# Gather stage of a graph layer on one Trainium2 core: VectorE makes a pick between two adds, the valid mask is folded into the scaling of keys and values, and ScalarE normalises the pairs' rows

## The reference

```python
xn = layernorm(x)
x = x + gcn(xn, edge_index, edge_weight) + mix(xn)     # both read xn
x = x + ffn(layernorm(x))                              # 8 experts, top 2
# gcn: per node the sum over its edges of weight * xw[source], then a two-layer head
# mix: q, k, v = split(xn @ w_qkv); k, v = ln(k), ln(v) by head
#      kv = k^T v / N by head (a 32x32 matrix); out = q @ kv; then a two-layer head
```

## Time and profile before

| | us |
|---|---|
| median of three runs | 4517.35 |
| profiled execution | 4502.67 |
| its span | 4500.9 |
| TensorE busy | 3399.5 (76%) |
| VectorE busy | 2931.0 (65%) |
| GpSimd busy | 2770.0 (62%) |
| ScalarE busy | 1429.0 (32%) |

### The profile page before, as it was taken

The page is one execution under the profiler, slowest core; times in us unless marked ns, Lnnn a source line. Parts: engine busy times, 40 slices in busy tenths (PEclk is TensorE's granted clock), DMA queues, the critical chain, the costliest instruction groups (busy, mean ns, idle before and its releaser), DMA issues. The chain is left out here.

```text
span 4500.9 us, 75623 instructions
## 1 busy us (share of the span) xinstructions
PE 3399.5 (76%) x20283; PEld 2597.3 (58%) x20283; DVE 2931.0 (65%) x7496; ACT 1429.0 (32%) x4439; POOL 2770.0 (62%) x2543
## 2 busy tenths in 40 slices
PE   7677777246777777777756777777777589999995
PEld 6455554243444444444435666566665479999885
DVE  8899998674565565655655555555555665555676
ACT  2455554440111111111002222222322255555442
POOL 0488888436666666666666666666666245555553
PEclk9678787557888888888868888888888799999998
DMA  2111111763333333333334444444446612222466
GB/s 76 17 3 3 3 3 3 239 228 116 110 108 111 110 112 108 111 110 111 109 89 119 128 131 131 130 130 132 128 130 121 139 46 70 68 70 68 148 217 215
DMA packets 285822, 472.50 MB, mean 105 GB/s; under 512 B 95011, under 2 KB 180778, under 8 KB 285743
## 3 DMA queue, kind: packets, MB, share of 16 engines
q0 software_dynamic: 140544, 273.69, 24.5%
q1 hardware_dynamic: 138047, 193.90, 12.7%
q10 hardware_dynamic: 7154, 3.99, 0.3%
HBM read 350.11 MB, written 123.70 MB: 105 GB/s over the span
## 5 line engine op out<-in xcount | busy, mean ns | idle before, releaser
L1621 POOL DMA_INDIRECT rows<-table,idx x1664 | 1675.1, 1007 | 815.5 <-issue 497.3
L1904 DVE TENSOR_TENSOR acc<-acc,ps_seg 128x256 f32 x1664 | 695.5, 418 | 955.5 <-remote 761.6
L2069 PE MATMUL ps_seg<-rows,pick 128*128 128x256 f32 x3328 | 997.3, 429 | 272.0 <-DVE acc L1904 182.0
L2069 PEld LDWEIGHTS ps_seg<-rows,pick 128*128 128x128 f32 x3328 | 660.4, 213 | 514.0 <-issue 404.6
L771 POOL DMA_INDIRECT records<-sort_rec,sort_addr x280 | 528.8, 1889 | 260.7 <-DVE sort_rec L874 158.7
L1746 DVE TENSOR_SCALAR pick<-iota_row,loc,ewt 128x128 f32<-128x128 f32 x1680 | 529.2, 363 | 5.6 <-remote 1.8
L2509 POOL DMA_INDIRECT y_rows<-arena,idx x212 | 249.8, 1178 | 290.0 <-DVE arena L2556 185.2
L2641 PE MATMUL ps_h<-arena,up_now 128*128 128x128 f32 x3392 | 417.8, 277 | 0.0
L2625 PE MATMUL ps_y<-down_now,arena 128*128 128x256 f32 x1696 | 401.4, 380 | 0.0
L2641 PEld LDWEIGHTS ps_h<-arena,up_now 128*128 128x128 f32 x3392 | 398.3, 193 | 1.9
L926 PE MATMUL ps_out<-acc 128*128 128x240 bf16 x1568 | 281.5, 364 | 142.0 <-DVE acc L860 141.9
(11 more groups left out here) (385 smaller groups left out, 5122.7 us busy)
## 6 DMA issues: line engine op xcount, KB each, us to landing
rows<-table,idx POOLq DMA_INDIRECT x1664
acc<-y_rows SPq DMA_DIRECT2D x28, 640.0 KB
xn<-xn_dram SPq DMA_DIRECT2D x100, 128.0 KB
table<-acc SPq DMA_DIRECT2D x98, 128.0 KB
xT_dram<-xT SPq DMA_DIRECT2D x98, 128.0 KB
xn<-xT_dram SPq DMA_DIRECT2D x49, 256.0 KB
skip<-skip_dram SPq DMA_DIRECT2D x49, 256.0 KB
x_rows<-acc SPq DMA_DIRECT2D x49, 256.0 KB
```

What stands on the lines that cost most here:

```text
L1621: pool.indirect_dma_start(out=rows[:, t, :], out_offset=None, in_=k.table, in_offset=bass.IndirectOffsetOnAxis(idx[:, h, t:t + 1], 0), bou ...
L1904: dve.tensor_tensor(here, here, sums(u), ALU.add).then_inc(added[u], 1)
L2069: last = pe.matmul(sums(t), pick[:, h, t, :], rows[:, t, :], start=True, stop=True)
```

## The change

On VectorE the order of picks and adds becomes pick, add, pick, add; the wait for the pair's sums stands ahead of its first add, behind the first pick. The multiplication by `valid` goes; the scaling takes it as a second factor, in one instruction with three operands. Normalising the pairs' rows goes from VectorE, at the end of a step, to ScalarE, in the next step between `aggregated` and `features`, as rows * rstd + shift, for which VectorE makes shift = -mean * rstd.

```diff
 def normalised(i):                                   # now ScalarE's
+    start_after(act, rows_out, 16 * i)
+    start_after(act, f_done, i)
+    act.wait_ge(shift_done, i + 1)
+    act.sem_inc(head_held, 1)
+    for h in both:
+        act.activation(xl[:, h:h + 1, :], k.acc[:, bass.ds(2 * i + h, 1), :], ACT.Identity,
+                       scale=rstd[:, h:h + 1], bias=shift[:, h:h + 1]).then_inc(xl_done, 1)
...
                         if due(i - 2):
+                            normalised(i - 2)
                             features(i - 2)
...
                 def inverses(m):
                     dve.wait_ge(k_sd, m + 1)
+                    start_after(dve, k_scaled, m)
                     dve.reciprocal(rs[:, :], sd[:, :]).then_inc(k_rs, 1)
-                def masked(m):
-                    dve.wait_ge(k_rs, m + 1)
-                    dve.tensor_scalar(rsv[:, :], rs[:, :], k.valid[:, bass.ds(m, 1)], None, ALU.mult).then_inc(k_rsv, 1)
-                def scaled(m, u):
-                    dve.wait_ge(k_rsv, m + 1)
                     dve.wait_ge(k_raw, m + 1)
                     start_after(dve, k_summed, m - 1)
-                    dve.tensor_tensor(kv_heads(u), by_head4(raw[:, u, :]),
-                                      rsv[:, :]..., ALU.mult).then_inc(k_scaled, 1)
+                    dve.scalar_tensor_tensor(
+                        out=kv_heads(u), in0=by_head4(raw[:, u, :]), scalar=k.valid[:, bass.ds(m, 1)],
+                        in1=rs[:, :]..., op0=ALU.mult, op1=ALU.mult).then_inc(k_scaled, 1)
...
                 def inverse(i):
                     dve.wait_ge(std_done, i + 1)
+                    start_after(dve, xl_done, 2 * i)
                     dve.reciprocal(rstd[:, :], std[:, :]).then_inc(rstd_done, 1)
-                def normalised(i):
-                    start_after(dve, rows_out, 16 * i)
-                    start_after(dve, f_done, i)
                     dve.wait_ge(rstd_done, i + 1)
                     dve.sem_inc(head_held, 1)
-                    for h in both:
-                        dve.tensor_scalar(xl[:, h:h + 1, :], k.acc[:, bass.ds(2 * i + h, 1), :], mv[:, h, 0:1],
-                                          rstd[:, h:h + 1], ALU.subtract, ALU.mult).then_inc(xl_done, 1)
+                    dve.scalar_tensor_tensor(out=shift[:, :], in0=mv[:, :, 0], scalar=-1.0, in1=rstd[:, :],
+                                             op0=ALU.mult, op1=ALU.mult).then_inc(shift_done, 1)
...
                     for t in range(STEP_TILES):
                         make_pick(1 - h, t)
+                        if t % 2 == 0:
+                            dve.wait_ge(summed_up[t // 2], n + 1)
+                        if t > 0:
+                            dve.wait_ge(added[t - 1], n + 1)
+                        else:
+                            start_after(dve, added[ALL_TILES], n)
+                        here = acc_row[:, bass.ds(places[t], D)]
+                        dve.tensor_tensor(here, here, sums(t), ALU.add).then_inc(added[t], 1)
                         if t % 2 == 0:
                             continue
-                        dve.wait_ge(summed_up[t // 2], n + 1)
-                        for u in (t - 1, t):
-                            if u > 0:
-                                dve.wait_ge(added[u - 1], n + 1)
-                            else:
-                                start_after(dve, added[ALL_TILES], n)
-                            here = acc_row[:, bass.ds(places[u], D)]
-                            dve.tensor_tensor(here, here, sums(u), ALU.add).then_inc(added[u], 1)
```

More of the change, by code:

```diff
@@ L1449, in gather_and_mix @@
         rstd = sb("rstd3", [P, 2])
+        shift = sb("shift3", [P, 2])
         wr = sb("wr", [P, DC, N_EXPERTS])
@@ L1455, in gather_and_mix @@
         rs = sb("rs", [P, 2 * HEADS])
-        rsv = sb("rsv", [P, 2 * HEADS])
         kv = sb("kv", [P, 2, 2 * DC, WIDE])
@@ L1497, in gather_and_mix @@
             k.sem(name) for name in "idx_done loci_done loc_done ewt_done gather_held".split())
-        (kv_consts, k_turned, k_xT, k_kv, k_raw, k_sq, k_ss, k_sd, k_rs, k_rsv, k_scaled, k_summed, k_all_summed) = (
-            k.sem(name) for name in ("kv_consts k_turned k_xT k_kv k_raw k_sq k_ss k_sd k_rs k_rsv k_scaled k_summed "
+        (kv_consts, k_turned, k_xT, k_kv, k_raw, k_sq, k_ss, k_sd, k_rs, k_scaled, k_summed, k_all_summed) = (
+            k.sem(name) for name in ("kv_consts k_turned k_xT k_kv k_raw k_sq k_ss k_sd k_rs k_scaled k_summed "
                                      "k_all_summed").split())
@@ L1503, in gather_and_mix @@
         (mix_hid, gelu_done, mix_out, h7_done, h7T_done, h7T_copied, gcn_hid, relu_done, all_out, x1_done, stats_done, mv_done,
-         std_done, rstd_done, xl_done, f_done, fT_copied, lg_done, lgb_done, eps2_made, head_held) = (
+         std_done, rstd_done, shift_done, xl_done, f_done, fT_copied, lg_done, lgb_done, eps2_made, head_held) = (
             k.sem("pair_" + name) for name in (
                 "mix_hid gelu_done mix_out h7_done h7T_done h7T_copied gcn_hid relu_done all_out x1_done stats_done mv_done "
-                "std_done rstd_done xl_done f_done fT_copied lg_done lgb_done eps2_made held").split())
+                "std_done rstd_done shift_done xl_done f_done fT_copied lg_done lgb_done eps2_made held").split())
         by_block = lambda a: a.rearrange("(t p) d -> p t d", p=P)
@@ L1683, in deviation, with normalised @@
                     act.activation(std[:, :], mv[:, :, 1], ACT.Sqrt, bias=eps2[:, :], scale=1.0 + EPS).then_inc(std_done, 1)
+                def normalised(i):
+                    start_after(act, rows_out, 16 * i)
[5 more added lines that the diff above has]
+                                       scale=rstd[:, h:h + 1], bias=shift[:, h:h + 1]).then_inc(xl_done, 1)
                 def features(i):
@@ L1765, in inverses, with scaled @@
                     dve.wait_ge(k_sd, m + 1)
+                    start_after(dve, k_scaled, m)
                     dve.reciprocal(rs[:, :], sd[:, :]).then_inc(k_rs, 1)
[L1768 removed]
+                def scaled(m, u):
                     dve.wait_ge(k_rs, m + 1)
[L1770 to L1773 removed]
                     dve.wait_ge(k_raw, m + 1)
                     start_after(dve, k_summed, m - 1)
[L1776 to L1778 removed]
+                    dve.scalar_tensor_tensor(
+                        out=kv_heads(u), in0=by_head4(raw[:, u, :]), scalar=k.valid[:, bass.ds(m, 1)],
+                        in1=rs[:, :].rearrange("p (c h) -> p c h", c=2 * DC).unsqueeze(3).to_broadcast(
+                            [P, 2 * DC, HEADS_PER_CHUNK, HEADC]), op0=ALU.mult, op1=ALU.mult).then_inc(k_scaled, 1)
                 g = k.k_gb[:, 0, :].unsqueeze(1).to_broadcast([P, HEADS_PER_CHUNK, HEADC])
@@ L1878, in beside @@
                         inverse(i - 1)
-                        normalised(i - 1)
                 def step(n, h, mode, base, q, turn):
@@ L1891, in step @@
                     for t in range(STEP_TILES):
+                        half, at = t // SLOT, t % SLOT
                         make_pick(1 - h, t)
-                        half, at = t // SLOT, t % SLOT
+                        if t % 2 == 0:
[6 more added lines that the diff above has]
+                        dve.tensor_tensor(here, here, sums(t), ALU.add).then_inc(added[t], 1)
                         if t % 2 == 0:
                             continue
-                        dve.wait_ge(summed_up[t // 2], n + 1)
-                        for u in (t - 1, t):
-                            if u > 0:
-                                dve.wait_ge(added[u - 1], n + 1)
-                            else:
-                                start_after(dve, added[ALL_TILES], n)
-                            here = acc_row[:, bass.ds(places[u], D)]
-                            dve.tensor_tensor(here, here, sums(u), ALU.add).then_inc(added[u], 1)
                         if mode == "kv" and live(base + half - 2):
@@ L1909, in step @@
                                 inverses(base + half - 2)
-                                masked(base + half - 2)
                             if at == 7:
```

2 lines of the change are left out of this document (removed).

## The result

The changed kernel takes 4526.44 us (median of nine runs, 4520.56 to 4532.31) against 4515.73 for the kernel before (nine runs, 4512.70 to 4520.52): a ratio of 1.0023, 95% interval [1.0014, 1.0032]. It is slower by 11 us. The prediction named 4492; the time lies in its range of 4445 to 4535, but on the other side of no change than forecast. The profiled execution's span went from 4500.9 to 4519.2 us.

What follows compares the result with a forecast made beforehand. Gathers were taken to bound the stage, with VectorE's freed time worth 0.2 us per us. The terms -24, -2, -17, +12, +2 gave -29, rounded to -25: from 4517.35 to 4492 us, range 4445 to 4535.

Steps and rivals of the forecast that it cites:

- What bounds the kernel: Expert stage: 1664 gathers need 2171 of 2489 us; VectorE is not the bound on average, but catching up sooner lengthens gather runs.
- The order, in VectorE's time: VectorE's picks and adds: alternating them takes a pair of tiles from 1.39 to 1.18 us, 1.7 us saved a step, 104 steps.
- The rival that rests on the rule: VectorE's adds: an add keeps VectorE 0.55 us whatever follows, so the new order saves nothing; 4523 us, chance 0.05.
- The mask: Steps with keys and values: 0.39 us saved a block, scaling 0.06 longer; net 0.66 us a step of VectorE's time.
- The turning of the rows: TensorE in pair steps: starts 0.85 us later behind ScalarE's normalising; costs 0 to 40 us, taken as 12.
- Behind the last gather +2: Last three pairs, with no gathers to hide behind: each pays 0.85 us for the later turning, +2 us.
- From VectorE's time to the kernel's: Whole stage: VectorE's freed time converted at 0.2 us per us; 24, 2 and 17 us saved, against 12 and 2 lost.
- The slope of 0.2 us per us: Steps with keys and values against plain ones: 3.8 us more on VectorE, 0.7 us longer, so 0.2 us per us.
- Its own signs: Forecast wrong if "remote" waits stay in number while VectorE's idle time grows by 170 us, or pair steps take over 24.2 us.
- "No change": Gathers: late words come whatever VectorE does, leaving the turning's 12 us or part of them; 4510 to 4526 us, chance 0.16.
- "Slower": Pair steps: TensorE's turning waits for ScalarE in each, without cover; 42 us less other gains, 4517 to 4559, middle 4535, chance 0.20.

## Why the prediction was wrong

- *What bounds the kernel.* Right in its main reading: the gathers set the stage, and VectorE is not the bound on average. The sentence behind it was the fault. That a VectorE which catches up sooner leaves the gathers "with more announced sums", so that their runs between stops get longer, was an argument without a row. The stops stayed (156 against 133), and with the order alone in a group with stops the gathers idled as long as before (812.0 and 815.5 us). Why a late word is not made up for by a VectorE that is quicker behind it was not shown; half the room between sums and adds was tried only where no word is late.
- *The order, in VectorE's time.* Right: 1.21 us a pair against the 1.18 that was counted. The Trainium skill's rule ("VectorE: DVE Perf Modes", section "The DRAIN you can't avoid"), as the prediction read it, would have left 1.39; the same section adds that a next instruction which is not held starts earlier, and the measured 1.21 goes with that. The 43.9 us with half the gathers show the gain to be real. The rival that rests on the rule gave 4523 and came nearer to the time than my forecast, but by luck: the new order does free the time, and the kernel has no use for it.
- *The mask.* Right in VectorE's time: 0.16 to the next pick (0.14 counted), and 0.75 for the scaling (0.74 counted). It was worth nothing that can be told in any run.
- *The turning of the rows.* Right. Counted 0.85 us later, measured 0.95. Its price was taken as 12 us in the pair steps out of 0 to 40, and normalising alone cost 11.8 (1173.8 less 1162.0), the changed kernel 12.9. That 12 met 11.8 is luck, as the 0.25 us a step was chosen and not counted. Without the gathers as cover it is 44.9, a little over the upper end of 40. Behind the last gather +2 was foreseen; with half the gathers it read 38.8 us before and 41.8 with normalising alone, which goes with that, and with all of them the traces spread by more than 2.
- *From VectorE's time to the kernel's.* This is the step that failed. The slope of 0.2 us per us carried 43 us of saving, and the measured value of the term is 0 within the noise: with stops, order alone 0.9996 and order and mask 1.0006, so that 177 us freed by the order gave 2 us and at most 6 of the 35 counted; and the other way, without stops, 464 us more on VectorE for 4 us. It was read from the steps with keys and values taking 0.7 us longer than plain ones, with 3.8 us more on VectorE. By the windows VectorE's busy time differs by 1.7 us a step and not by 3.8 (696.4/50 less 73.6/6, the folding in the latter), and those steps differ in everything else too, TensorE's and ScalarE's work among it, and six plain steps with random stops fix no difference of 0.7. Without stops the two kinds take 21.0 and 20.9 us a step (1050.3/50 and 125.4/6). With the term at 0 the sum of the prediction is 12 + 2, or 4531 from the median that it started from and 4530 from the one measured beside the change; the time was 4526. Its own signs said so too: the pair steps took 24.5 us, over the 24.2 that it set as a limit, and the "remote" waits did not fall, though VectorE's idle time ahead of the adds grew by 122 us and not by 170.
- *The rivals.* "No change" had the right mechanism (the stops come whatever VectorE does, and 12 us or part of them are left) and a chance of 0.16 for it. "Slower" asked for a slope under 0.15 together with the whole delay passed on. The first half held, the second only where the gathers were thinned; its 4535 was 9 us too high. I had weighed the slope as if the row behind it were as good as those behind the counts of VectorE's time.

## What to carry to other kernels

Time freed on an engine has no price of its own: it is worth what the pacing engine then does sooner, which was nothing here while the gathers set the pace and 0.88 us of 1.7 a step once they did not. A slope read from two stages that differ in more than that engine's load is not a measurement; adding load to the engine and timing it is. And work moved from a waiting engine to a link of the chain that another engine waits for can be a loss even where the first one is the busier of the two; here 0.9 us a step, of which a quarter showed with the gathers in the way and all of it without them.

## What the runs showed of the hardware

- The same kernel takes 4515 us in one group of runs and 4210 in another, and the whole difference lies in this stage: 2489 us against 2182 from first to last gather, with gathers of 1.00 us in both. In the slower kind the word of finished sums arrives late: in the sample VectorE goes on at 1536.17 and GpSimd at 1536.84, and ScalarE at 1536.00 by the same timeline, and of the 133 gathers held up, the 126 that waited for a sum went on 3.1 to 19.6 us after its last matmul had ended. In the other kind no gather's wait ended so. With half the gathers left out such waits all but cease in the slower kind too, which points to the gathers' rate or the transfers that they start; but much else changes with them, TensorE's clock among it. What makes it was not settled. Chip 2 of the record ran in both kinds within ten minutes, so it is more likely a state that lasts for some time than a property of a chip.
- A gather that starts during a VectorE instruction that reads two operands from SBUF takes longer: 1.55 us instead of 1.00 for one that starts with a scaling of 0.68, and none of it for reductions of one operand and adds from PSUM. These extensions summed to 4.4 to 12.8 us from trace to trace, 0.1 to 0.3% of this kernel; with the same instructions in these steps they were 4.7 in one trace and 9.2 in another.
- The granted clock in the pair steps was 0.86 with stops, 0.96 without them (kernel before in the second kind) and 1.00 with half the gathers.
- ScalarE's pass over 128x256 with scale and bias from columns took 1.08 us for two, the pass with the scale alone 0.91.
